# Last layer of a four-layer recurrent model: wide projections among the head pairs, decays ahead of the second query copy, two groups of state inputs on GpSimd

## The chip, the cores and the metric

One core of one Trainium2 chip runs the whole kernel, all in float32. The metric is the time of one execution on the device in microseconds (us). TensorE is PE in the rows, its weight loads are PEld, VectorE is DVE, ScalarE is ACT, GpSimd is POOL, and SyncE, which only issues transfers here, is SP.

## The reference

Sixteen sequences of 256 rows and 128 columns go through four layers, each of which is `x = x + s * silu(f)`. Only the last layer is touched. There `xn = layernorm(x)`, `s` is a state-space block and `f` is a small transformer block:

```
# s: d_inner = 256, 16 states, rank 64
u, z   = split(xn @ in_proj.T)               # the wide projections
xs     = silu(causal_conv4(u) + conv_b)
dt,B,C = split(xs @ x_proj.T)                # 64 + 16 + 16 rows
delta  = softplus(softplus(dt @ dt_proj + dt_b) + dt_b)
state  = exp(delta * -exp(A_log)) * state + (delta * xs) * B   # one step of time
s      = ((state . C + xs * D) * silu(z)) @ out_proj.T
# f: 16 heads of 8, 8 experts of 512, top 2
q,k,v  = xn @ Wqkv + b ; q,k rotated
x1     = layernorm(xn + softmax(q k.T / sqrt(8)) v @ Wo + bo)
f      = layernorm(x1 + sum of the two chosen experts of x1)
```

## The kernel before

The last layer takes the second half of the time. It works on one sequence at a time, 16 in all, in a loop of four passes with four sequences written out in each. Every engine has its program in the order in which it is written, and engines meet at semaphores; nothing else decides the order. While sequence n runs, the parts of n+1 that depend on its input alone are made ahead. One round has these stages:

- **Pairs.** The 16 heads are taken in 8 pairs. For pair p PE makes the transposed scores (`scoresT`, line 2316, nine rows of the array in use), ACT takes their exponential (`exp_scores`, line 2518), and PE multiplies by the values, one block of two pairs at a time (`heads_out`, line 2374). ACT also makes the decays, exp(delta * A), that the scans need: 16 states in four groups of four, two halves (i) of the 256 channels, so eight calls of `decays` (line 2510), each with four activations. `exp_scores(n, p)` ends with one of them. PE turns the next sequence's normed rows here (`turn_x`, line 2247, behind pair 5). Meanwhile DVE scans groups 0 and 1 (`scan`, line 2811) and multiplies by C (`times_c`, line 2821).
- **Between.** The heads' outputs are turned (line 2412), DVE divides by the sums, then follow the output projection (line 2423), a layer norm on DVE and POOL that gives `x1`, the turning of `x1` (line 2430), and the router. PE also has `project_uz` here: the causal convolution as four shifted products for u (line 2257) and z (line 2261).
- **Experts.** Eight experts, up (line 2386) and down (line 2397); DVE adds them and does groups 2 and 3 of the state. `project_dt` makes dt for n+1.
- **Heads.** q and k of n+1 are turned (line 2284), the scores are made (line 2302), and DVE takes the maximum of each row, in four blocks (`heads_max`, line 2780). The negative maximum is written beside q, and q is turned again with it (`copy_qm`, line 2471), so that the exponential needs no bias. Around it DVE and ACT make the double softplus (`softplus_sum`, line 2739) and du = delta * xs (line 2755).
- **Closing.** DVE makes ym, the output of the scan after the gate (its last instruction is line 2918, which raises `ym_ready`), then `state_input` for groups 0 and 1 of n+1 (line 2787, two halves each), and then waits for th_z (tanh of f's half) and for `s_taken`, ACT's copy of the output product (line 2585). With both it updates x (lines 2923, 2926 and 2929). The next round opens with `norm_stats` of the new rows, `scan(0, 0)`, and `norm_rows` (line 2687), which waits for the inverse deviation that POOL takes as a power (line 94).

`scan` works in place on `st[i]`, which `state_input` has filled with du times B. B and C come as rows that SP spreads over all partitions into `bct`; `bct_read` tells SP that a group's slot is free again.

Of the kernel before, what the change touches and what calls it, by code (L numbers as in the profile page):

```python
# [2081 lines left out]
def layer3(nc, c):  # L2082
    w = c.w3
    with ExitStack() as ctx:
# [140 lines left out]
        delta_ready = sem("delta_ready")  # L2225
        dA_ready = sem("dA_ready")
# [14 lines left out]
        def _(pe):  # L2241
# [12 lines left out]
            def project_uz():  # L2254
                for i in range(CI):
                    for k in range(DCONV):
                        done = nc.tensor.matmul(bank[:, 2, i * T:(i + 1) * T], u_projT[:, i, k, :], xpad[:, k:k + T],
                                                start=(k == 0), stop=(k == DCONV - 1))
                done.then_inc(u_in_psum, 1)
                for i in range(CI):  # L2260
                    done = nc.tensor.matmul(bank[:, 3, i * T:(i + 1) * T], z_projT[:, i, :], xnT,
                                            start=True, stop=True)
                done.then_inc(z_in_psum, 1)
# [8 lines left out]
            def project_dt(m):  # L2272
                pe.wait_ge(xdbl_ready, m + 1)
                pe.wait_ge(zg_ready, m + 1)
# [83 lines left out]
            project_uz()  # L2358
# [3 lines left out]
            with pe.Fori(0, NSEQ // 4) as m:  # L2362
                for q in range(4):
# [26 lines left out]
                    def down(e):  # L2390
                        pe.wait_ge(hid_ready, 2 * E3 * n + 2 * e + 2)
                        pe.wait_ge(acc_taken, E3 * n + e + 1)
                        if e == 1:
                            pe.wait_ge(logits_taken, n + 1)
# [20 lines left out]
                    pe.wait_ge(xnT_ready, n + 2)  # L2415
                    qkv_rows(0)
                    pe.wait_ge(y_ready, n + 1)
                    for a in range(TILES):
                        done = nc.tensor.transpose(bank[:, 4, a * P:(a + 1) * P], y[:, a, :], c.ident[:, :])
                    done.then_inc(yT_in_psum, 1)  # L2420
                    pe.wait_ge(yT_ready, n + 1)
                    for a in range(TILES):
                        done = nc.tensor.matmul(bank[:, 5, a * D:(a + 1) * D], yT[:, a * P:(a + 1) * P], w.o[:, :],
                                                start=True, stop=True)
                    done.then_inc(o_in_psum, 1)
                    project_uz()
                    qkv_rows(1)
                    pe.wait_ge(x1_ready, n + 1)
                    for a in range(TILES):
                        done = nc.tensor.transpose(bank[:, 4, a * P:(a + 1) * P], x1[:, a, :], c.ident[:, :])  # L2430
                    done.then_inc(x1T_in_psum, 1)
                    pe.wait_ge(x1T_ready, n + 1)
                    for a in range(TILES):
                        done = nc.tensor.matmul(bank[:, 5, a * E3:(a + 1) * E3], x1T[:, a * P:(a + 1) * P], w.g[:, :],
# [28 lines left out]
        def _(act):  # L2463
# [16 lines left out]
            def silu_uz(m, par):  # L2480
                act.wait_ge(u_in_psum, m + 1)
                for i in range(CI):
                    done = v.activation(xs[:, par, i, :], bank[:, 2, i * T:(i + 1) * T], ACT.Silu,
# [524 lines left out]
```

## Time and profile before

| | |
|---|---|
| median of 3 runs | 2950.62 us (2947.14 to 2953.3) |
| the profiled execution | 2951.83 us, span 2950.1 us |
| mean granted TensorE clock over the span | 0.854 |
| busy: PE, DVE, ACT, POOL | 85%, 79%, 57%, 11% of the span |

The span is the time between the first and the last instruction, so 1.7 us lie around it. The clock is given as the share of 2.4 GHz: 1.00 is 2.4 GHz and 0.50 is 1.2 GHz, and values between are stretches with some of both.

### The profile page before, as it was taken

The page shows a single profiled execution, that of the slowest core. Times are in us where ns is not written, and L with a number is a line of the kernel's source. Part 1 is how long each engine was busy: PE and PEld are TensorE (multiplying, and loading weights), DVE is VectorE, ACT ScalarE, POOL GpSimd, SP SyncE. Part 2 cuts the span into 40 slices and gives each one's busy share as a digit, 9 for nine tenths or more (in the row PEclk, how much of TensorE's full clock was granted, in tenths as well). Part 3 has the DMA queues.
Part 4 walks back from the last instruction along what each step waited for, and adds up shares of the span by engine and source line. Part 5 has one row for each costly group of instructions (what it writes and reads, how often), then busy time and mean ns, then how long its engine had stood idle before and what let it go on. Part 6 is the DMA issues. An engine that isn't in the chain of part 4 may idle for free. (4 is left out here: it accounts for less than half of the span.)

```text
span 2950.1 us, 55763 instructions
## 1 busy us (share of the span) xinstructions
PE 2500.4 (85%) x18940; PEld 1896.2 (64%) x18940; DVE 2327.4 (79%) x6064; ACT 1689.7 (57%) x3432; POOL 336.4 (11%) x357
## 2 busy tenths in 40 slices
PE   1899998899999999776649888888988888888886
PEld 1666666677777777655636666666665666666665
DVE  1899998788788888675257888888888888888887
ACT  1677776556565566443326565655656565565654
POOL 0000000000000000033121111111111111111111
PEclk9999999899999999888858777788776778877777
DMA  7000000000000000210214323343433334443334
GB/s 220 2 0 0 0 0 0 1 2 0 1 0 1 0 1 0 64 27 27 58 55 106 93 73 86 88 108 94 108 87 75 88 89 107 95 102 84 76 91 110
DMA packets 86524, 163.77 MB, mean 56 GB/s; under 512 B 18856, under 2 KB 45617, under 8 KB 86321
## 3 DMA queue, kind: packets, MB, share of 16 engines
q0 software_dynamic: 20480, 62.93, 11.2%
q1 hardware_dynamic: 64640, 98.15, 10.3%
q8 instruction: 94, 1.54, 0.2%
q14 instruction: 110, 0.89, 0.1%
q10 hardware_dynamic: 1200, 0.27, 0.1%
HBM read 92.60 MB, written 9.99 MB: 35 GB/s over the span
## 5 line engine op out<-in xcount | busy, mean ns | idle before, releaser
L1140 ACT ACTIVATE b_neg<-b_neg,b_nmax 128x128 f32<-128x128 f32 (+1 forms) x512 | 190.9, 444 | 205.6 <-DVE b_nmax L1294 205.6
L2548 ACT ACTIVATE d_probs<-l_bank,w_b 128x256 f32<-128x256 f32 x512 | 210.8, 469 | 155.6 <-PE l_bank L2386 153.3
L2811 DVE TENSOR_TENSOR_SCAN d_state<-w,d_state 128x1024 f32<-128x1024 f32 x128 | 290.9, 2284 | 3.8 <-issue 3.4
L2386 PE MATMUL l_bank<-xnT,w_w 128*128 128x256 f32 x1024 | 245.1, 382 | 13.8 <-ACT d_probs L2548 13.8
L2397 PE MATMUL l_bank<-w_w,d_probs 128*128 128x128 f32 x2048 | 252.6, 276 | 0.0
L2397 PEld LDWEIGHTS l_bank<-w_w,d_probs 128*128 128x128 f32 x2048 | 244.9, 192 | 11.7 <-ACT d_probs L2548 5.3
L2316 PE MATMUL l_bank<-w 9*128 9x256 f32 x1040 | 208.8, 669 | 25.5 <-ACT w L2471 18.9
L2510 ACT ACTIVATE w<-d_delta,w_A_log 128x255 f32<-128x255 f32 x520 | 220.2, 498 | 0.0
L94 POOL TENSOR_TENSOR ln_rstd<-ln_var_eps,minus_half 128x2 f32<-128x2 f32 x51 | 70.6, 1384 | 1293.1 <-DVE ln_var_eps L88 1293.1
L2386 PEld LDWEIGHTS l_bank<-xnT,w_w 128*128 128x128 f32 x1024 | 184.7, 190 | 40.5 <-ACT d_probs L2548 20.7
L2316 PEld LDWEIGHTS l_bank<-w 9*128 9x128 f32 x1040 | 123.7, 320 | 96.0 <-issue 32.3
L1294 DVE CUSTOM_DVE_ANT_0 b_neg<-l_bank,causal 128x128 f32<-128x128 f32 (+1 forms) x512 | 151.9, 353 | 32.3 <-PE l_bank L989 16.4
L2780 DVE TENSOR_REDUCE d_qk<-l_bank 128x8 f32<-128x2048 f32 x68 | 152.7, 2288 | 5.5 <-PE l_bank L2302 4.5
L2821 DVE TENSOR_TENSOR d_state<-d_state,d_bct 128x1024 f32<-128x1024 f32 x128 | 151.1, 1222 | 6.3 <-issue 2.7
L1015 PEld LDWEIGHTS l_bank<-down,b_fused 128*128 128x128 f32 x1024 | 123.9, 191 | 50.1 <-issue 29.8
L2302 PE MATMUL l_bank<-w 8*128 8x256 f32 x1088 | 113.1, 562 | 48.5 <-ACT w L2477 25.0
L1015 PE MATMUL l_bank<-down,b_fused 128*128 128x128 f32 x1024 | 148.2, 288 | 6.9 <-DVE b_y L1326 6.3
L2787 DVE TENSOR_TENSOR d_state<-d_bct,d_du 128x1024 f32<-128x1024 f32 x132 | 153.9, 1218 | 0.1
L2616 POOL DMA_DIRECT2D d_state<-d_state x96 | 85.6, 1046 | 588.9 <-DVEq L2823 476.5
L2374 PE MATMUL l_bank<-d_probs,d_vaug 128*32 128x256 f32 x1024 | 123.9, 634 | 30.9 <-ACT d_probs L2518 30.9
L2471 ACT ACTIVATE w<-l_bank 128x1024 f32<-128x1024 f32 x34 | 34.8, 1024 | 198.8 <-PE l_bank L2284 198.8
L2518 ACT ACTIVATE d_probs<-l_bank 128x1024 f32<-128x1024 f32 x130 | 132.1, 1016 | 24.1 <-PE l_bank L2316 24.1
(404 smaller groups left out, 5699.2 us busy)
## 6 DMA issues: line engine op xcount, KB each, us to landing
d_bct<-l_bc SPq DMA_DIRECT2D x132, 512.0 KB, 4.0
d_state<-d_state POOLq DMA_DIRECT2D x96, 512.0 KB, 6.7
d_state<-d_state POOLq DMA_DIRECT2D x32, 256.0 KB, 4.0
x_sorted<-x SPq DMA_DIRECT2D x1, 2560.0 KB, 16.7
w<-in_L_ffn_w_dram SPq DMA_DIRECT2D x1, 2048.0 KB, 10.3
w_w<-in_L_ffn_W_dram SPq DMA_DIRECT2D x1, 2048.0 KB
c2e_xg<-x_sorted SPq DMA_DIRECT2D x16, 128.0 KB
y_sorted<-c2e_yo SPq DMA_DIRECT2D x16, 128.0 KB, 1.8
```

What stands on the lines that cost most here:

```text
L1015: done = nc.tensor.matmul(bank[:, 7, a * D:(a + 1) * D], fused[:, e % 2, f * T + a * P:f * T + (a + 1) * P], c.down1[:, e, f, :], start=(f ...
L1140: done = nc.scalar.activation(neg[:, slot, cols], neg[:, slot, cols], ACT.Exp, bias=nmax[:, slot, a:a + 1], scale=-1.0)
L1294: done = v.tensor_tensor_reduce(neg[:, slot, lo:hi], bank[:, 1 + b, lo:hi], c.causal[:, lo:hi], -SCALE, 3e38, ALU.add, ALU.min, nmax[:, sl ...
L2316: done = nc.tensor.matmul(back[:, 2 * (p % 2) + i, j * T:(j + 1) * T], kT[own, blk, j * P:(j + 1) * P], qT[own, blk, :], start=True, stop= ...
L2386: done = nc.tensor.matmul(bank[:, b, i * T:(i + 1) * T], w.w1[:, e, k * P:(k + 1) * P], x1T[:, :], start=True, stop=True)
L2397: done = nc.tensor.matmul(bank[:, 4 + e % 2, a * D:(a + 1) * D], hid[:, e % 2, k, a * P:(a + 1) * P], w.w2[:, e, k, :], start=(k == 0), st ...
L2510: done = v.activation(dA[i][:, g % (NG - 1), k, 1:T], delta[:, i, 1:T], ACT.Exp, scale=negA[:, i, SG * g + k:SG * g + k + 1])
L2548: done = v.activation(hid[:, e % 2, k, :], bank[:, b, i * T:(i + 1) * T], ACT.Gelu, bias=w.b1[:, e, k:k + 1])
L2780: v.tensor_reduce(qk[:, :, 0, GR * blk:GR * (blk + 1), HD3].rearrange("p a h -> p h a"), banks.rearrange("p h (a t) -> p h a t", a=TILES), ...
L2787: done = v.tensor_tensor(st[i][:, SG * g:SG * (g + 1), :], bct[:, g, :, :], du[:, i, :].unsqueeze(1).to_broadcast([P, SG, T]), ALU.mult)
L2811: done = v.tensor_tensor_scan(group, dA[i][:, g % (NG - 1), :, :].rearrange("p m t -> p (m t)"), group, 0.0, ALU.mult, ALU.add)
L2821: done = v.tensor_tensor(group, group, bct[:, g, :, :], ALU.mult)
```

## The change

Four things are done to the last layer.

1. `project_uz` is cut into `project_u(0)`, `project_u(1)` and `project_z`, which stand behind the scores of pairs 5, 6 and 7. They write to banks 4 and 5 of PSUM instead of 2 and 3, and other small results trade places with them. `turn_x`, whose result they need, moves from behind pair 5 to behind pair 3.
2. The four calls of `decays` for groups 0 and 1 stand in front of `copy_qm`. Of the eight pairs only every second one still carries a call, for groups 2 and 3.
3. For that, `delta` is made sooner: the second `softplus_sum` moves from behind the fourth block of `heads_max` to behind the first.
4. `state_input` of groups 0 and 1 goes from DVE to POOL, where it waits for `ym_ready`, since it overwrites what ym is made of. `scan(0, 0)` and `scan(1, 0)` wait for it.

```diff
-            def project_uz():
+            def project_u(i):
+                for k in range(DCONV):
+                    done = nc.tensor.matmul(bank[:, 4, i * T:(i + 1) * T], u_projT[:, i, k, :], xpad[:, k:k + T],
+                                            start=(k == 0), stop=(k == DCONV - 1))
...
@@ PE, pairs
+                        if k == 3:
+                            turn_x(n + 1, 1 - par)
                         if k == 5:
-                            turn_x(n + 1, 1 - par)
+                            pe.wait_ge(xnT_ready, n + 2)
+                            project_u(0)
+                        if k == 6:
+                            project_u(1)
+                        if k == 7:
+                            project_z()
...
@@ PE, behind the output projection
                     done.then_inc(o_in_psum, 1)
-                    project_uz()
                     qkv_rows(1)
...
@@ ACT
                              scale=float(HD3) ** -0.5).then_inc(probs_ready, 1)
-                decays(n, p // 2, p % 2)
+                if p % 2:
+                    decays(n, 2 + p // 4, p // 2 % 2)
...
                     log_part(n + 1, 1)
+                    for k in range(4):
+                        decays(n + 1, k // 2, k % 2)
                     copy_qm(n + 1)
...
@@ POOL
+            def state_input(m, g):
+                pool.wait_ge(bct_loaded[g], 32 * m + 16)
+                pool.sem_inc(pool_step, 1)
+                for i in range(CI):
+                    nc.gpsimd.tensor_tensor(st[i][:, SG * g:SG * (g + 1), :], bct[:, g, :, :],
+                                            du[:, i, :].unsqueeze(1).to_broadcast([P, SG, T]), ALU.mult)
+                nc.gpsimd.drain().then_inc(bct_read[g], 1)
+                pool.sem_inc(input_ready, 1)
...
                     inner_power(2 * n + 2)
+                    pool.wait_ge(du_ready, n + 2)
+                    pool.wait_ge(ym_ready, n + 1)
+                    for g in range(2):
+                        state_input(n + 1, g)
...
@@ DVE
             def third_part(m, par):
-                softplus_sum(m, 1)
-                v.tensor_tensor(du[:, :, :], delta[:, :, :], xs[:, par, :, :], ALU.mult)
+                v.tensor_tensor(du[:, :, :], delta[:, :, :], xs[:, par, :, :], ALU.mult).then_inc(du_ready, 1)
...
                         dve.wait_ge(dA_ready, CI * NG * n + CI * g + i + 1)
+                        if g < 2 and i == 0:
+                            dve.wait_ge(input_ready, 2 * n + g + 1)
...
                         heads_max(n + 1, blk)
+                        if blk == 0:
+                            softplus_sum(n + 1, 1)
...
-                    for g in range(2):
-                        state_input(n + 1, g)
                     dve.wait_ge(th_z_ready, n + 1)
```

**PE in the pairs.** Before, from the output product of the scan (line 2325) to the turning of the heads' outputs (line 2412). `l_bank` is PSUM, line 2316 is `scoresT`, 2374 is `heads_out`, 2247 is `turn_x`.

```order
L2325 MATMUL l_bank<-d_out_projT,d_ym 128x128 x4
L2316 MATMUL l_bank<-w 128x256 x4
L2374 MATMUL l_bank<-d_probs,d_vaug 32x256 x8
L2316 MATMUL l_bank<-w 128x256 x4
L2316 MATMUL l_bank<-w 128x256 x4
L2374 MATMUL l_bank<-d_probs,d_vaug 32x256 x8
L2316 MATMUL l_bank<-w 128x256 x4
L2247 MATMUL l_bank<-ident,d_xn 128x128 x2
L2316 MATMUL l_bank<-w 128x256 x4
L2374 MATMUL l_bank<-d_probs,d_vaug 32x256 x8
L2316 MATMUL l_bank<-w 128x256 x4
L2374 MATMUL l_bank<-d_probs,d_vaug 32x256 x8
```

The same place in the changed kernel, from behind the first `heads_out`; its lines 2321, 2381 and 2249 are the 2316, 2374 and 2247 of before, and 2258 and 2265 are u and z.

```order
L2321 MATMUL l_bank<-w 128x256 x4
L2249 MATMUL l_bank<-ident,d_xn 128x128 x2
L2321 MATMUL l_bank<-w 128x256 x4
L2381 MATMUL l_bank<-d_probs,d_vaug 32x256 x8
L2321 MATMUL l_bank<-w 128x256 x4
L2258 MATMUL l_bank<-d_xpad,d_u_projT 128x256 x4
L2321 MATMUL l_bank<-w 128x256 x4
L2381 MATMUL l_bank<-d_probs,d_vaug 32x256 x8
L2258 MATMUL l_bank<-d_xpad,d_u_projT 128x256 x4
L2321 MATMUL l_bank<-w 128x256 x4
L2265 MATMUL l_bank<-d_xpad,d_z_projT 128x256 x2
L2381 MATMUL l_bank<-d_probs,d_vaug 32x256 x8
```

`turn_x` now stands between the scores of pairs 3 and 4, which were neighbours, and ten wide products stand between the later ones.

**POOL from the closing of a round into the next.** `until` is the layer norm's small memory, `ln_rstd` the inverse deviation that `norm_rows` needs; lines 2617 and 2618 of the changed kernel are 2598 and 2599 of before.

```order
+L2617 REGISTER_ALU
+L2618 TENSOR_TENSOR until<-until,minus_half 128x2
+L2623 ISA
+L2626 TENSOR_TENSOR d_state<-d_bct,d_du 128x1024 x4
 L93 REGISTER_ALU
 L94 TENSOR_TENSOR ln_rstd<-ln_var_eps,minus_half 128x2
```

The four products of `state_input` now stand ahead of the power for `norm_rows` in POOL's program.

**ACT in heads and closing.** The changed kernel, from the second softplus to the copy for `s_taken` (2604); 2524 is `decays`, 2485 `copy_qm`, 2532 `exp_scores`.

```order
L2514 ACTIVATE d_dneg<-d_dneg 128x512
L2516 ACTIVATE d_dneg<-d_dneg 128x512
L2524 ACTIVATE w<-d_delta,w_A_log 128x255 x16
L2485 ACTIVATE w<-l_bank 128x1024
L2600 ACT_TABLE_LOAD
L2600 ACTIVATE d_x<-same_head 128x256
L2532 ACTIVATE d_probs<-l_bank 128x1024
L2532 ACTIVATE d_probs<-l_bank 128x1024
L2524 ACTIVATE w<-d_delta,w_A_log 128x255 x4
L2604 ACTIVATE xnT<-l_bank 128x256
```

Sixteen of the activations stand ahead of `copy_qm`, where there were none, and four instead of eight stand between the first exponential and the copy for `s_taken`.

## Rows read from the trace of the kernel before

**Rows 1.** Stretches of one round: busy PE, PEld, DVE, ACT, POOL, granted clock, DMA.

```profile
2500.49:2586.51 86.02, 74.88 (x476) 55.73 (x476) 73.96 (x139) 50.45 (x98) 12.38 (x12) 0.76 0.38 93
2502.53:2523.03 20.50, 18.63 (x115) 9.06 (x114) 18.29 (x21) 19.33 (x40) 2.65 (x1) 0.50 0.14 52
2533.82:2567.57 33.75, 32.47 (x214) 28.99 (x212) 28.19 (x71) 19.57 (x42) 5.30 (x6) 1.00 0.59 146
```

**Rows 2.** Timeline of PE in that round: start, us, [idle before <-releaser].

```profile
2502.53 2.08 PE L2316 MATMUL l_bank<-w 9*128 9x256 f32 x8
2504.54 1.94 PE L2374 MATMUL l_bank<-d_probs,d_vaug 128*32 128x256 f32 x16
2506.40 2.45 PE L2316 MATMUL l_bank<-w 9*128 9x256 f32 x16
...
2513.48 0.69 PE L2247 MATMUL l_bank<-ident,d_xn 128*128 128x128 f32 x2
2514.10 2.08 PE L2316 MATMUL l_bank<-w 9*128 9x256 f32 x8
...
2521.17 1.94 PE L2374 MATMUL l_bank<-d_probs,d_vaug 128*32 128x256 f32 x16 [1.12 <-ACT d_probs L2518]
```

**Rows 3.** Timeline of ACT around the closing.

```profile
2497.24 1.02 ACT L2471 ACTIVATE w<-l_bank 128x1024 f32<-128x1024 f32 x1 [9.82 <-PE l_bank L2284]
...
2501.36 1.69 ACT L2510 ACTIVATE w<-d_delta,w_A_log 128x255 f32<-128x255 f32 x4
2502.96 1.00 ACT L2518 ACTIVATE d_probs<-l_bank 128x1024 f32<-128x1024 f32 x1
...
2505.46 0.37 ACT L2585 ACTIVATE xnT<-l_bank 128x256 f32<-128x256 f32 x1
```

**Rows 4.** Timeline of DVE, heads, closing and the next round's opening.

```profile
2486.18 9.00 DVE L2780 TENSOR_REDUCE d_qk<-l_bank 128x8 f32<-128x2048 f32 x4
2495.10 0.68 DVE L2739 SCALAR_TENSOR_TENSOR d_delta<-d_dv,d_dneg 128x512 f32<-128x512 f32 x1
...
2500.38 4.63 DVE L2787 TENSOR_TENSOR d_state<-d_bct,d_du 128x1024 f32<-128x1024 f32 x4
2505.93 0.42 DVE L2923 SCALAR_TENSOR_TENSOR d_y<-d_x,same_head 128x256 f32<-128x256 f32 x1 [0.92 <-ACT xnT L2585]
...
2508.28 2.29 DVE L2811 TENSOR_TENSOR_SCAN d_state<-w,d_state 128x1024 f32<-128x1024 f32 x1
2511.09 0.60 DVE L2687 TENSOR_SCALAR d_xn<-x,ln_meanvar,ln_rstd 128x128 f32 x2 [0.52 <-POOL ln_rstd L94]
...
2525.83 0.37 DVE L2845 RECIPROCAL until<-l_bank 128x16 f32<-128x16 f32 x2 [2.27 <-PE l_bank L2412]
```

**Rows 5.** Timeline of POOL in the same round.

```profile
2508.41 2.65 POOL L94 TENSOR_TENSOR ln_rstd<-ln_var_eps,minus_half 128x2 f32<-128x2 f32 x1 [23.08 <-DVE ln_var_eps L88]
...
2530.71 0.71 POOL L2599 TENSOR_TENSOR until<-until,minus_half 128x2 f32<-128x2 f32 x1 [4.73 <-DVE until L2764]
2531.39 0.72 POOL L2595 TENSOR_TENSOR xn<-d_xn,w_bo 128x256 f32<-128x256 f32 x1
```

**Rows 6.** POOL's groups by form, whole span: count, busy us, mean ns.

```profile
L721 POOL TENSOR_TENSOR a_hbias<-a_hneg,a_hrstd 128x2 f32<-128x2 f32 x16 | 3.2, 197 | 2.3
```

**Rows 7.** DVE's L2769, beside POOL's L2595 and without it.

```profile
2531.45 1.00 DVE L2769 TENSOR_SCALAR same_head<-same_head,until 128x128 f32<-128x128 f32 x2 [0.31 <-POOL until L2599]
...
2582.52 0.59 DVE L2769 TENSOR_SCALAR same_head<-same_head,until 128x128 f32<-128x128 f32 x2
```

**Rows 8.** L2257, product for u: before the first round, and in a round.

```profile
1516.97:1518.25 1.28, 1.28 (x4) 1.01 (x3) 0.50 0.00 0
2528.85:2532.31 3.46, 3.46 (x16) 2.84 (x16) 1.00 0.98 250
```

**Rows 9.** PE between two stages: busy, then the granted clock, DMA, GB/s.

```profile
2525.30:2528.70 3.40, 2.93 (x10) 0.50 0.96 181
2529.70:2533.80 4.10, 4.10 (x19) 1.00 0.62 178
```

More of the change, by code:

```diff
@@ L2252, in qkv_rows, with project_z @@
                     .then_inc(qkv_in_psum, 1)
-            def project_uz():
-                for i in range(CI):
[L2256 to L2261, printed above, removed]
+            def project_u(i):
+                for k in range(DCONV):
+                    done = nc.tensor.matmul(bank[:, 4, i * T:(i + 1) * T], u_projT[:, i, k, :], xpad[:, k:k + T],
+                                            start=(k == 0), stop=(k == DCONV - 1))
+                if i == CI - 1:
+                    done.then_inc(u_in_psum, 1)
+            def project_z():
+                for i in range(CI):
+                    done = nc.tensor.matmul(bank[:, 5, i * T:(i + 1) * T], z_projT[:, i, :], xnT,
                                             start=True, stop=True)
@@ L2273, in project_dt @@
                 pe.wait_ge(xdbl_ready, m + 1)
-                pe.wait_ge(zg_ready, m + 1)
+                if later(m):
+                    pe.wait_ge(logits_taken, m)
                 for i in range(CI):
@@ L2418, in _ @@
                     for a in range(TILES):
-                        done = nc.tensor.transpose(bank[:, 4, a * P:(a + 1) * P], y[:, a, :], c.ident[:, :])
+                        done = nc.tensor.transpose(bank[:, 2, a * P:(a + 1) * P], y[:, a, :], c.ident[:, :])
                     done.then_inc(yT_in_psum, 1)
@@ L2429, in _ @@
                     for a in range(TILES):
-                        done = nc.tensor.transpose(bank[:, 4, a * P:(a + 1) * P], x1[:, a, :], c.ident[:, :])
+                        done = nc.tensor.transpose(bank[:, 2, a * P:(a + 1) * P], x1[:, a, :], c.ident[:, :])
                     done.then_inc(x1T_in_psum, 1)
@@ L2433, in _ @@
                     for a in range(TILES):
-                        done = nc.tensor.matmul(bank[:, 5, a * E3:(a + 1) * E3], x1T[:, a * P:(a + 1) * P], w.g[:, :],
+                        done = nc.tensor.matmul(bank[:, 3, a * E3:(a + 1) * E3], x1T[:, a * P:(a + 1) * P], w.g[:, :],
                                                 start=True, stop=True)
@@ L2482, in silu_uz @@
                 for i in range(CI):
-                    done = v.activation(xs[:, par, i, :], bank[:, 2, i * T:(i + 1) * T], ACT.Silu,
+                    done = v.activation(xs[:, par, i, :], bank[:, 4, i * T:(i + 1) * T], ACT.Silu,
                                         bias=w.conv_b[:, i:i + 1])
@@ L2486, in silu_uz @@
                 act.wait_ge(z_in_psum, m + 1)
-                v.activation(zg[:, par, :, :].rearrange("p i t -> p (i t)"), bank[:, 3, :], ACT.Silu)\
+                v.activation(zg[:, par, :, :].rearrange("p i t -> p (i t)"), bank[:, 5, :], ACT.Silu)\
                     .then_inc(zg_ready, 1)
@@ L2534, in _ @@
             log_part(0, 1)
+            for k in range(4):
+                decays(0, k // 2, k % 2)
             copy_qm(0)
@@ L2578, in _ @@
                     log_part(n + 1, 1)
+                    for k in range(4):
+                        decays(n + 1, k // 2, k % 2)
                     copy_qm(n + 1)
@@ L2629, in _ @@
                     inner_power(2 * n + 2)
+                    pool.wait_ge(du_ready, n + 2)
+                    pool.wait_ge(ym_ready, n + 1)
+                    for g in range(2):
+                        state_input(n + 1, g)
         @block.sync
@@ L2798, in _ @@
                 heads_max(0, blk)
+                if blk == 0:
+                    softplus_sum(0, 1)
             third_part(0, 0)
-            v.drain()
-            for g in range(2):
-                state_input(0, g)
             v.drain()
@@ L2854, in _ @@
                     dve.wait_ge(resid_ready, n + 1)
-                    v.tensor_tensor(rows[:, :, :], bank[:, 5, 0:TILES * D].rearrange("p (a d) -> p a d", d=D),
+                    v.tensor_tensor(rows[:, :, :], bank[:, 3, 0:TILES * D].rearrange("p (a d) -> p a d", d=D),
                                     resid[:, :, :], ALU.add).then_inc(rows_ready, 1)
@@ L2918, in _ @@
                     v.tensor_tensor(ym[:, :, :], ym[:, :, :], zg[:, par, :, :], ALU.mult).then_inc(ym_ready, 1)
-                    for g in range(2):
-                        state_input(n + 1, g)
                     dve.wait_ge(th_z_ready, n + 1)
```

24 lines of the change are left out of this document (16 added, 8 removed).

## The prediction

> **What bounds the kernel now.** I first cut one round of the last layer out of the trace (the table of stretches), then read the timelines of PE, ACT, DVE and POOL over it, since the average over the span hides which engine is last in which stage. A round is 86.02 us, and over it PE is busy 74.88, DVE 73.96, ACT 50.45 and POOL 12.38 us [rows 1]. PE and DVE are both nearly full, so the reader should ask stage by stage who waits for whom, not who is busiest.
>
> Let 2500.5 us, the end of ym, be 0. Pairs: from the third scores to the end of the last `heads_out` is 20.50 us. PE is busy 18.63 of it and ACT 19.33, PE's clock is at 0.50 (1.2 GHz) all through, and PE's last wait, 1.12 us, is for ACT [rows 1, 2]. DVE is the one with room: it waits 2.27 us for the turned outputs at 25.3 [rows 4]. So the stretch from 0 to there is set by PE and ACT in turn, and DVE's work beside it is hidden by 2.27 us. Experts: PE is busy 32.47 of 33.75 us at clock 1.00 and bounds [rows 1]. Heads: DVE's four maxima run without a gap for 9.00 us and bound [rows 4]. Closing: DVE makes the state inputs in 4.63 us and then still waits 0.92 us for ACT's copy [rows 4].
>
> **The change part by part.**
>
> Earlier `softplus_sum` (0.68 us, about 0.7 with the drain behind it [rows 4]): it goes in between the maxima and is missing behind them, so ym ends when it did, but the last maximum comes 0.7 later, and with it the second turning, `copy_qm`, and the first scores. Cost at the start of the pairs: +0.7.
>
> Half of the decays ahead of `copy_qm`: a call takes 1.60 us (start of one to start of what follows, 2501.36 to 2502.96 [rows 3]), four take 6.4. `delta` is ready at 2486.18 + 2.25 + 0.7 = 2489.1 (one of four maxima is 2.25), so they end at 2495.5. `copy_qm` began at 2497.24 after 9.82 us of idle [rows 3], and would now at 2497.9. The idle hides them with 2.4 us over. Free.
>
> Fewer decays in the closing: ACT's copy for `s_taken` had two calls ahead of it and now has one: -1.6 + 0.7 puts its end at about 2504.9 where it was 2505.8 [rows 3]. DVE therefore starts the update of x 0.9 earlier, though 4.63 us of work left it. The rest becomes idle: what was removed from DVE here covered a wait.
>
> State inputs on POOL. No such product of 1024 elements is in the trace. POOL takes 0.72 us for 256 elements, one operand spread [rows 5], and 0.197 for 2 [rows 6], so 2.06 ns an element and 2.3 us for 1024. Bounds: 1.2 us, DVE's price for it (4.63/4 [rows 4]), and 2.9, four times 0.72. I take 2.3. Group 0 then runs from 0.1 to 4.7, and with drain and waits group 1 from 4.9 to 9.5, if nothing holds it. Behind these in POOL's program stands the power for `norm_rows` [rows 5], behind that `norm_rows`, and behind that `turn_x` on PE. SP's loads of C wait for the same products to be done with B: they start 2.6 (group 0) and up to 6 us (group 1) later, while the scans and `times_c` that need them move by about 4 themselves. I count nothing for them.
>
> Does DVE hold POOL up, and POOL DVE? The power on two elements took 2.65 us under a scan that ran from 2508.28 to 2510.57 (it ended at 2511.06, 0.49 behind the scan), but 0.71 where no scan ran [rows 4, 5]. The other way round, DVE's two scalings took 1.00 us beside POOL's addition and 0.59 without it [rows 7]. So each waits the other out. The Trainium skill, "SBUF — State Buffer", "SBUF: two separate sides", says that the port pair of the two is an exclusive lock for the whole instruction, against DVE instructions with two inputs from SBUF as well. By that rule the trace agrees in both directions, and the sum is the one with holding, below; by a reading in which POOL never holds such a DVE instruction the sum would be 4.1 us a round less.
>
> With holding: DVE's update of x is three instructions of 0.43, the first at 4.5. It waits for POOL's second product (4.7), runs to 5.2, POOL takes 2.3, the second runs, POOL takes 2.3, the third ends at 10.6. Statistics and issue up to the scan are 1.0 (2505.93 to 2508.28 less three starts of 0.45), the scan 2.3: about 14.0. The power ends 0.5 later and two scalings take 0.6 [rows 4]: the normed rows are there at 15.1, against 11.2 before. Without holding: POOL free at 9.5, power 0.7, scalings 0.6, and some issue, so 11.0. The scan stands in front anyway.
>
> When does PE want them? Before, `turn_x` ran at 13.0 [rows 2] and waited for nothing. Now it stands behind pair 3: third scores at 2.0 + 0.7 = 2.7, +2.0, `heads_out` +1.9, scores +2.0 = 8.6. PE stands still for 6.5 us (2.4 without holding).
>
> The rest of the pairs on PE, start to start: `turn_x` 0.6, scores 2.0 each, `heads_out` 1.9 each [rows 2]. Adjacent scores of pairs 3 and 4 overlapped (both in 2.45 plus a wait), which `turn_x` between them ends. The new products: four instructions at clock 0.50 begin within 1.28 us, so 0.427 each, against 0.216 at 1.00 [rows 8]. u is 16 of them, z 4: 3.4 for each half of u and 1.7 for z at 1.2 GHz. From `turn_x`: 0.6 + 2.0 + 1.9 + 2.0 = 6.5; then 3.4 + 2.0 + 1.9 + 3.4 + 2.0 + 1.7 + 1.9 = 16.3. End at 15.1 + 22.8 = 37.9. Before it was 22.5. That is +15.4 with the clock low throughout.
>
> The clock. The grant rose right behind a stretch in which PE was busy 2.93 of 3.40 us with turnings and products over the full array [rows 9], and stays at 0.50 through nine-row scores and `heads_out` [rows 1]. u(0) and u(1) are such full stretches of 3.4 us, but each is followed by nine-row scores. If the grant rises behind u(0), the 12.9 us behind it halve: -6.4; behind u(1), -2.5; never, 0. I take half, a quarter and a quarter: -3.8.
>
> Between: u and z leave a place where PE was busy 4.10 of 4.10 us [rows 9]. It delayed the turning of x1 by 0.4, so -0.4, and no more, since DVE's layer norm ran beside it. But only one product of 0.7 is left there, so the clock may be low when the experts begin. PE would lose half of a stretch as long as that from the first full-array work at 23.3 to the rise at 28.2, 4.9/2 = 2.4. I take half: +1.2. Removing u and z from the experts' stage saves nothing, as they were not in it.
>
> Sum for a round: 15.4 (this holds +0.7 and the wait of 6.5) - 3.8 - 0.4 + 1.2 = +12.4. Sixteen rounds: +198. On the profiled execution, 2951.8 us (1.2 above the median of the runs shown), it gives 3150.
>
> **The rivals.**
>
> *The two engines do not hold each other* (POOL's products only delay the power behind them). The wait at `turn_x` is 2.4: 12.4 - 4.1 = 8.3 a round, 3085. For it: the trace shows DVE held only with its scalings, not with a two-input instruction. Against it: the power held by the scan, all of its length.
>
> *The clock rises at the first wide product and stays* (-6.4, and +0 for the experts). 15.4 - 6.4 - 0.4 = 8.6, 3089; with the first rival too 4.5, 3024. For it: 3.4 us of full-array work. Against: the scores behind it. Its opposite, a clock that stays low in the pairs and starts low in the experts, is 17.4, 3230. The Trainium skill, "TensorE: Matmul & The Clock Gate", "HAM oscillation — how this bites in real kernels", describes such falling back when short bursts alternate with pauses; with only that, the sum would be near the 3230, and no run here shows it yet for the pairs.
>
> *Faster: the relief of DVE and ACT is what counts.* The wide products go into PE's waits. DVE's 4.63 a round off the whole is 74 us, 2877. For it: DVE is as full as PE over a round, and ACT's decays stand between the exponentials that PE waits for. Against: PE has 1.9 us of idle in 20.5 in the pairs, and gets 8.5 at 1.2 GHz. It decides if the last `heads_out` ends by 22.5, which needs about 2.4 GHz from the first scores and normed rows by 8.6.
>
> *No change.* The savings and the costs cancel: 2951.
>
> **How the numbers follow.** The forecast 0.55, no holding 0.15, the clock early (with or without holding) 0.15, all low 0.05, faster 0.06, same 0.04. Range 3040 to 3220: it takes in both middle rivals with 3089, most of the case with both (3024 lies outside), and of the high case all but the worst. About 0.2% is what a measurement of this kernel can tell from no change: faster 0.06, same 0.04, slower 0.90.
>
> **What the profile after would show.** Right: POOL's line 2626 with 4 instructions a round of about 2.3 us, some longer where a scan or the update holds them; `turn_x` (2249) with some 6 us of idle before it, released by the normed rows; the update of x split by POOL's products; u and z at about 0.43 an instruction in half of the cases; a pairs stretch above 30 us. ACT's sixteen decays inside the idle time of the maxima. Wrong if POOL's products take under 1.5 us, if the clock is 1.00 through the pairs, if `turn_x` waits under 2 us, or if the experts' stretch begins at 1.00 in all rounds; each takes its term out of the sum.

## The result, and the profile after

The changed kernel takes 3148.22 us (median of 4, 3146.94 to 3151.67), the kernel before in the same runs 2949.72. The ratio is 1.0674, interval 1.0655 to 1.0692: slower by 198 us. The profiled execution of the changed kernel has a span of 3149.9 us. From one end of ym to the next, a round took 86.50 us on average before (15 intervals) and takes 98.81 now, +12.3.

The round looked at from here on starts at 2534.57, the end of ym. Its stretches, against those of [rows 1] (us, busy PE, PEld, DVE, ACT, POOL, granted clock, DMA share, GB/s):

```profile
2534.57:2633.75 99.18, 79.03 (x480) 57.83 (x478) 70.73 (x135) 50.94 (x98) 21.95 (x16) 0.74 0.33 81
2537.25:2569.24 31.99, 26.00 (x135) 14.30 (x134) 17.75 (x18) 13.06 (x26) 11.63 (x7) 0.57 0.27 66
2569.24:2579.21 9.97, 3.54 (x19) 2.07 (x19) 6.79 (x19) 3.94 (x8) 1.40 (x2) 0.96 0.16 53
2579.21:2614.61 35.40, 34.93 (x213) 31.00 (x214) 28.58 (x71) 19.66 (x41) 5.06 (x6) 0.91 0.54 136
2614.61:2633.75 19.14, 11.88 (x102) 8.64 (x104) 17.60 (x27) 12.05 (x23) 1.51 (x2) 0.63 0.16 28
```

The pairs (second row) went from 20.50 to 31.99 us; PE is idle for 6 of them and ACT for 19. The experts (fourth row) went from 33.75 to 35.40, and their clock from 1.00 to 0.91. Those two stretches hold the loss. The timeline of PE over the pairs and the place behind them answers to [rows 2]:

```profile
2537.25 2.08 PE L2321 MATMUL l_bank<-w 9*128 9x256 f32 x8
2539.25 1.94 PE L2381 MATMUL l_bank<-d_probs,d_vaug 128*32 128x256 f32 x16
2541.12 2.08 PE L2321 MATMUL l_bank<-w 9*128 9x256 f32 x8
2549.12 0.69 PE L2249 MATMUL l_bank<-ident,d_xn 128*128 128x128 f32 x2 [5.93 <-DVE d_xn L2722]
...
2555.62 3.78 PE L2258 MATMUL l_bank<-d_xpad,d_u_projT 128*128 128x256 f32 x8
2559.33 2.08 PE L2321 MATMUL l_bank<-w 9*128 9x256 f32 x8
2561.34 1.94 PE L2381 MATMUL l_bank<-d_probs,d_vaug 128*32 128x256 f32 x16
2563.21 2.78 PE L2258 MATMUL l_bank<-d_xpad,d_u_projT 128*128 128x256 f32 x8
2565.92 1.13 PE L2321 MATMUL l_bank<-w 9*128 9x256 f32 x8
...
2579.21 0.69 PE L2444 MATMUL l_bank<-ident,d_x 128*128 128x128 f32 x2 [4.58 <-DVE d_x L2809]
2580.37 1.02 PE L2448 MATMUL l_bank<-w_g,xnT 128*128 128x8 f32 x4 [0.47 <-ACT xnT L2584]
2581.25 3.76 PE L2393 MATMUL l_bank<-xnT,w_w 128*128 128x256 f32 x8
```

`turn_x` waits 5.93 us for the normed rows. u(0) takes 3.7 us; within u(1) the clock rises, and the scores behind it take 1.13 us instead of 2.08. The turning of x1 comes after 4.58 us of idle, and the first product of the experts takes 3.76 us where the ones behind it take 1.89. What POOL and DVE do meanwhile answers to [rows 4, 5]:

```profile
2534.90 4.67 POOL L2626 TENSOR_TENSOR d_state<-d_bct,d_du 128x1024 f32<-128x1024 f32 x2 [15.58 <-DVE d_ym L2955]
2540.60 6.83 POOL L2626 TENSOR_TENSOR d_state<-d_bct,d_du 128x1024 f32<-128x1024 f32 x2 [1.02 <-issue]
2547.74 0.69 POOL L94 TENSOR_TENSOR ln_rstd<-ln_var_eps,minus_half 128x2 f32<-128x2 f32 x1 [0.32 <-issue]
```
```profile
2539.22 0.64 DVE L2958 SCALAR_TENSOR_TENSOR d_y<-d_x,same_head 128x256 f32<-128x256 f32 x1 [4.65 <-ACT xnT L2604]
...
2541.66 1.43 DVE L88 TENSOR_SCALAR ln_var_eps<-ln_meanvar 128x2 f32<-128x2 f32 x1
2543.01 2.28 DVE L2846 TENSOR_TENSOR_SCAN d_state<-w,d_state 128x1024 f32<-128x1024 f32 x1
2548.47 0.60 DVE L2722 TENSOR_SCALAR d_xn<-x,ln_meanvar,ln_rstd 128x128 f32 x2 [3.18 <-POOL ln_rstd L94]
...
2571.37 0.37 DVE L2880 RECIPROCAL until<-l_bank 128x16 f32<-128x16 f32 x2 [10.38 <-PE l_bank L2428]
```

POOL's first two products take 4.67 us, undisturbed. The second pair takes 6.83: the scan of 2.28 us ran inside it. DVE is idle for 4.65 us in the closing, where the state inputs stood, and for 10.38 later.

### The profile page after: what moved, and what is told of

It is laid out like the page before. It is cut to its first block, busy times and chain, and to the rows that moved or that the text cites. A ratio compares the mean times of both kernels' runs of the same rounds, so it can differ in the third digit from the quotient of the medians.

```text
span 3149.9 us, 55927 instructions
## 1 busy us (share of the span) xinstructions
PE 2559.7 (81%) x18940; PEld 1927.7 (61%) x18940; DVE 2269.3 (72%) x5996; ACT 1702.6 (54%) x3444; POOL 499.9 (16%) x425
## 4 chain that ended last, share of the span: by engine, by line
PE 19%; issue 10%; DVE 9%; DVEq 5%; POOL 4%; POOLq 3%; ACT 1%; ACTq 0%
PE l_bank L2393 8%; PE l_bank L2406 7%; DVE d_qk L2814 4%; POOLq L2628 3%; POOL d_state L2626 3%; DVEq L2852 2%; DVE d_state L2856 1%; DVEq L2858 1%; DVE d_state L2846 1%; POOL d_state L2647 1%; PE l_bank L2272 1%; DVE same_head L2803 1%; PE l_bank L2281 1%; POOL ln_rstd L94 1%; PE l_bank L2448 1%
## 5 line engine op out<-in xcount | busy, mean ns | idle before, releaser
L2393 PE MATMUL l_bank<-xnT,w_w 128*128 128x256 f32 x1024 | 272.6, 414 | 0.0
L2321 PE MATMUL l_bank<-w 9*128 9x256 f32 x1040 | 218.9, 633 | 23.8 <-ACT w L2485 18.9
L2626 POOL TENSOR_TENSOR d_state<-d_bct,d_du 128x1024 f32<-128x1024 f32 x68 | 187.1, 2770 | 299.0 <-DVE d_ym L2955 248.1
L2393 PEld LDWEIGHTS l_bank<-xnT,w_w 128*128 128x128 f32 x1024 | 204.7, 209 | 27.6
L94 POOL TENSOR_TENSOR ln_rstd<-ln_var_eps,minus_half 128x2 f32<-128x2 f32 x51 | 47.3, 927 | 904.1 <-DVE ln_var_eps L88 899.9
L1294 DVE CUSTOM_DVE_ANT_0 b_neg<-l_bank,causal 128x128 f32<-128x128 f32 (+1 forms) x512 | 152.0, 353 | 34.7 <-PE l_bank L989 18.8
L997 PE MATMUL l_bank<-b_xnT,gating 128*128 128x256 f32 x512 | 135.0, 387 | 3.3 <-DVE b_gated L1311 3.3
L1003 PE MATMUL l_bank<-b_xnT,up 128*128 128x256 f32 x512 | 133.1, 383 | 0.0
```

The lines of the kernel that those rows point to most:

```text
L1294: done = v.tensor_tensor_reduce(neg[:, slot, lo:hi], bank[:, 1 + b, lo:hi], c.causal[:, lo:hi], -SCALE, 3e38, ALU.add, ALU.min, nmax[:, sl ...
L2321: done = nc.tensor.matmul(back[:, 2 * (p % 2) + i, j * T:(j + 1) * T], kT[own, blk, j * P:(j + 1) * P], qT[own, blk, :], start=True, stop= ...
L2393: done = nc.tensor.matmul(bank[:, b, i * T:(i + 1) * T], w.w1[:, e, k * P:(k + 1) * P], x1T[:, :], start=True, stop=True)
L2626: nc.gpsimd.tensor_tensor(st[i][:, SG * g:SG * (g + 1), :], bct[:, g, :, :], du[:, i, :].unsqueeze(1).to_broadcast([P, SG, T]), ALU.mult)
```

## The experiments

The changed kernel and the kernel before were first taken apart part by part; then single terms were tested. All ratios are to the kernel before in the same runs. "Round" and the places in it are medians over the 15 rounds of each profiled execution, in us behind the end of ym; "low" is the time at 1.2 GHz up to the last `heads_out`, and within the experts (from the turning of x1 to the turning of q and k).

| kernel | ratio (interval) | round | normed rows | wait at `turn_x` | last `heads_out` | experts | low: pairs, experts |
|---|---|---|---|---|---|---|---|
| before | 1 | 86.1 | 11.2 | 0 | 22.6 | 33.8 | 22.6, 0 |
| changed | 1.0674 (1.0655 to 1.0692) | 98.9 | 14.5 | 5.9 | 34.7 | 35.5 | 30.2, 6.3 |
| only_pool | 1.0080 (1.0063 to 1.0097) | 87.9 | 14.4 | 1.4 | 24.1 | 33.9 | 24.1, 0 |
| only_decays | 1.0028 (1.0018 to 1.0037) | 86.9 | 10.4 | 0 | 23.3 | 34.0 | 23.3, 0 |
| only_wide | 1.0480 (1.0463 to 1.0498) | 95.6 | 11.2 | 3.3 | 31.4 | 35.5 | 26.9, 6.3 |
| undo_pool | 1.0346 (1.0329 to 1.0363) | 92.2 | 10.4 | 1.8 | 27.8 | 35.6 | 20.2, 6.6 |
| gap_filled | 1.0607 (1.0562 to 1.0651) | 98.8 | 14.5 | 5.9 | 35.8 | 34.1 | 32.7, 0 |
| pairs_filled | 1.0318 (1.0300 to 1.0335) | 92.4 | 14.5 | 0.7 | 27.4 | 36.0 | 13.7, 7.2 |
| power_first | 1.0708 (1.0687 to 1.0728) | 99.4 | 14.7 | 6.2 | 34.9 | 35.4 | 30.4, 6.1 |
| split_groups | 1.0567 (1.0549 to 1.0584) | 96.3 | 12.4 | 3.8 | 32.2 | 36.0 | 27.5, 7.3 |
| late_wide | 1.0115 (1.0098 to 1.0132) | 88.6 | 10.4 | 0 | 26.1 | 34.1 | 22.2, 0 |
| warm_pairs | 0.9963 (0.9950 to 0.9975) | 85.4 | 10.2 | 0 | 22.9 | 34.1 | 13.7, 0 |
| warm_decays | 0.9890 (0.9873 to 0.9906) | 83.9 | 10.2 | 0 | 20.3 | 34.0 | 14.2, 0 |
| fill_only | 0.9970 (0.9957 to 0.9983) | 85.5 | 11.1 | 0 | 22.2 | 33.8 | 18.7, 0 |

**only_pool.** Part 4 of the diff put on the kernel before, nothing else.

> The kernel before with part 4 alone: POOL makes the state inputs of groups 0 and 1. Theory: the products come in front of the power for norm_rows and exclude scan and update, so the normed rows are there at about 14.5 us behind the end of ym instead of 11.2. turn_x stands at 13.0 here, so PE waits 1.5 to 2 us in a round: +24 to +32 us, ratio 1.008 to 1.011. Rival 'POOL's part is what costs': +8 or more in a round, ratio over 1.04. Rival 'relief of DVE counts': ratio 0.975.

1.0080, as the theory has it. The normed rows come 3.2 us later; since `turn_x` stands at 13.0 there, 1.4 us are left as a wait, and that is the loss. Neither rival fits. POOL's part is small by itself, because more than half of its lateness falls before PE asks. In the changed kernel PE waits for the rows in any case, and more of the lateness counts: 5.9 us of wait against 3.3 in only_wide, although the pairs start 0.7 later.

**only_decays.** Parts 2 and 3 on the kernel before.

> The kernel before with parts 2 and 3 alone: decays of groups 0 and 1 ahead of copy_qm, softplus sooner. Theory: pairs start 0.7 us later and PE at 1.2 GHz then paces them alone (18.6 us of work and about 1.5 of waits for exponentials), so a round stays within -0.3 to +0.6 us: ratio 0.998 to 1.003. Rival 'ACT's decays pace the pairs': -1 us or more in a round, ratio under 0.995.

1.0028: a small loss, the 0.7 us by which the last maximum and with it the pairs start later. That ACT has four calls of decays less in the pairs gave nothing.

**only_wide.** Part 1 on the kernel before.

> The kernel before with part 1 alone: wide projections and turn_x in the pairs. Theory: turn_x waits 2.5 to 3 us for the normed rows at 11.2, behind it PE needs 20 us (as in the changed kernel), so heads_out ends at 31.3 instead of 22.6; the experts start at a low clock (+1.7), the place between gives 0.7 back: +9.7 in a round, ratio 1.053 (1.045 to 1.060). Rival 'the products fit into PE's waits': under 1.01.

1.0480, inside the range. `turn_x` waits 3.3 us even with POOL's products absent, since the normed rows stand behind `scan(0, 0)` in any case. The rival (under 1.01) is out. This part alone makes 71% of the loss.

**undo_pool.** The changed kernel without part 4.

```diff
@@ POOL
-                    for g in range(2):
-                        state_input(n + 1, g)
...
@@ DVE, behind ym
+                    for g in range(2):
+                        state_input(n + 1, g)
```

> The changed kernel with the state inputs back on DVE. Theory: normed rows at 10.4 to 11, turn_x waits 2 to 2.5 us instead of 5.9, all else as in the changed kernel: +9.1 in a round against before, ratio 1.049 (1.042 to 1.055), that is 3.5 to 4 us a round faster than the changed kernel. Rival 'POOL's part is what costs': ratio under 1.02. Rival 'no holding, POOL is harmless': ratio as the changed kernel's, 1.067.

1.0346, under the range that I gave, and away from both rivals. The wait is 1.8, a little under what I expected, and from `turn_x` to the last `heads_out` it takes 17.3 us, not 20.1. The timeline shows where:

```profile
2203.78 0.69 PE L2247 MATMUL l_bank<-ident,d_xn 128*128 128x128 f32 x2 [1.84 <-DVE d_xn L2704]
...
2210.28 3.53 PE L2256 MATMUL l_bank<-d_xpad,d_u_projT 128*128 128x256 f32 x8
2213.74 1.13 PE L2319 MATMUL l_bank<-w 9*128 9x256 f32 x8
```

Here the clock rises at the end of u(0), in the changed kernel in the middle of u(1) in most rounds. So the removal of POOL's part gave 4.1 us by the shorter wait and 2.8 by the clock. The second is no property of the part: it depends on when the same products run, and in the two rounds of 96.2 us of the changed kernel, where the clock also rises at the end of u(0), the stretch takes 17.2 us with POOL's part in place. What single parts cost (1.7 + 0.7 + 9.4 = 11.8 us of a round by medians) is near the whole (12.8), but not a sum that can be relied on to 3 us.

**gap_filled.** Tests the low clock at the start of the experts.

```diff
                     done.then_inc(o_in_psum, 1)
+                    for _ in range(5):
+                        nc.tensor.matmul(bank[:, 7, 0:3 * D], xnT[:, P:2 * P], wqkv, start=True, stop=True)
                     qkv_rows(1)
```

> The changed kernel with the product for the second half of q, k, v made six times instead of once, in the place that u and z left behind the output projection (the copies rewrite the same values, so no result changes). They take about 3.9 us of the 5.4 that PE has there. Theory: the low clock at the start of the experts (6.3 us at 1.2 GHz in each round) comes from that empty place; with it filled the clock stays at 2.4 GHz, the stretch from the turning of x1 to the turning of q and k goes from 35.4 to 33.8 us, and a round is 1.6 us shorter: -26 us against the changed kernel, ratio to before 1.058. Rival 'the clock falls there for another reason': no change, 1.067.

The mechanism is confirmed: the stretch that answers to the experts has no time at 1.2 GHz in any round, and takes 34.06 us in the one shown.

```profile
2262.34:2296.40 34.06, 32.53 (x213) 29.05 (x213) 28.51 (x71) 19.39 (x41) 4.79 (x6) 1.00 0.55 141
```

The gain in time, 0.7% of the time before, measures this less well, since the rise in the pairs moved too. Ten rounds are 98.7 to 99.3 us long: there the last `heads_out` came later (35.8 against 34.7), with 32.6 to 33 us at 1.2 GHz up to it, and took most of the gain back. Five are 95.2 to 95.8, with 25.5 to 26 us at 1.2 GHz.

**pairs_filled.** Tests the price of the low clock in the pairs.

```diff
                         if k == 3:
+                            for _ in range(6):
+                                nc.tensor.matmul(bank[:, 5, T:2 * T], z_projT[:, 0, :], xnT, start=True, stop=True)
                             turn_x(n + 1, 1 - par)
```

> The changed kernel with six extra products over the full array (z's first half, into columns that nobody reads until they are written again) ahead of turn_x, 5.1 us at 1.2 GHz in a wait of 5.8. Theory: the clock rises at about the moment turn_x starts. If it holds through the nine-row scores, the stretch from turn_x to the last heads_out goes from 20.1 us to 12 to 13, a round is 7 us shorter, ratio 1.029; if the scores take it down again before u(0), it rises again behind u(0) as in undo_pool (17.3 us), 2 to 4 us shorter, ratio 1.045 to 1.056. Rival 'the low clock does not matter there, exponentials or the normed rows pace the pairs': under 1 us, ratio 1.065 or more.

1.0318: more work on PE, and 105 us less than the changed kernel. From `turn_x` to the last `heads_out`:

```profile
2310.10:2322.83 12.73, 12.66 (x102) 7.72 (x102) 11.34 (x7) 7.45 (x14) 0.19 (x1) 1.00 0.00 1
```

In this round the clock rose just ahead of `turn_x` and held through the nine-row scores; the same products take 12.73 us at 1.00 and 20.1 in the changed kernel. So it is in 11 of the 15 rounds, and there the first of my two cases is the right one. In the other four the clock fell again at 16.3 to 17.4 us behind ym, among the scores, and the stretch took 16.0 to 19.2. This execution took 3055.55 us, the three others 3041.43 to 3043.67.

**power_first.** Is it POOL's queue, or the holding?

```diff
@@ POOL, top of the round
-                    norm_power(nc, c, s, n + 1)
...
@@ POOL, end of the round
-                    for g in range(2):
-                        state_input(n + 1, g)
+                    state_input(n + 1, 0)
+                    norm_power(nc, c, s, n + 2)
+                    state_input(n + 1, 1)
```

> The changed kernel with the power for norm_rows between POOL's two groups instead of behind both (the order in its program; nothing is left out). Theory 'place in POOL's queue and holding': the power runs at about 7.4 or is held by the scan until 9.6, normed rows at 10 to 12 instead of 14.5, the second group of state inputs then alternates with scan(0, 1) and times_c(0), hidden by DVE's 10 us of idle time before the turned outputs. turn_x waits 1.5 to 3 instead of 5.8: a round 3 to 4 us shorter, and up to 3 more if the clock then rises a step earlier as in undo_pool: ratio 1.035 to 1.050. Rival 'holding alone': the products hold DVE's update and scan wherever they stand, normed rows at 13 or later, ratio over 1.058.

My theory fell and the rival stands: 1.0708, normed rows at 14.7. DVE:

```profile
2449.88 2.29 DVE L2847 TENSOR_TENSOR_SCAN d_state<-w,d_state 128x1024 f32<-128x1024 f32 x1
2452.69 4.66 DVE L2723 TENSOR_SCALAR d_xn<-x,ln_meanvar,ln_rstd 128x128 f32 x2 [0.52 <-POOL ln_rstd L94]
```

and POOL, in the same round:

```profile
2449.94 2.72 POOL L94 TENSOR_TENSOR ln_rstd<-ln_var_eps,minus_half 128x2 f32<-128x2 f32 x1 [2.43 <-DVE ln_var_eps L88]
2452.63 4.63 POOL L2626 TENSOR_TENSOR d_state<-d_bct,d_du 128x1024 f32<-128x1024 f32 x2
```

The power is done 10.2 us behind ym and not 13.9 as in the changed kernel, and the two scalings that it releases, 0.60 us of work, take 4.66, the length of POOL's second group (4.63). The order in POOL's program changed only which instruction was held.

**split_groups.** Does POOL also hold a DVE product with two inputs?

```diff
@@ DVE
                     v.tensor_tensor(ym[:, :, :], ym[:, :, :], zg[:, par, :, :], ALU.mult).then_inc(ym_ready, 1)
+                    state_input(n + 1, 1)
@@ POOL
-                    for g in range(2):
-                        state_input(n + 1, g)
+                    state_input(n + 1, 0)
```

> The changed kernel with group 1 of the state inputs back on DVE (2.4 us, in the closing, where DVE waits 4.65), group 0 on POOL at the same time. Theory 'they hold each other': DVE's two products and POOL's two start together and alternate; POOL's pair takes 6 to 7 us instead of 4.67, or DVE's products some 3.5 us instead of 1.22 each, the update of x starts at about 6 to 7. The power then follows the group at 8 to 10, normed rows at 11 to 12.5: 2 to 3.5 us a round shorter than the changed kernel, ratio 1.040 to 1.055. Rival 'no holding': both groups done by 5, each instruction at its own length, normed rows at 10.5, ratio as undo_pool's, 1.035.

Ratio 1.0567, a little above my range. DVE's and POOL's rows:

```profile
2414.77 4.51 DVE L2819 TENSOR_TENSOR d_state<-d_bct,d_du 128x1024 f32<-128x1024 f32 x2
2419.51 2.27 DVE L2959 SCALAR_TENSOR_TENSOR d_y<-d_x,same_head 128x256 f32<-128x256 f32 x1 [0.23 <-ACT xnT L2604]
```
```profile
2415.18 6.32 POOL L2626 TENSOR_TENSOR d_state<-d_bct,d_du 128x1024 f32<-128x1024 f32 x2 [15.57 <-DVE d_ym L2955]
```

DVE's two products take 4.51 us instead of 2.3 (four took 4.63 [rows 4]), POOL's 6.32 instead of 4.67, and the first instruction of the update 2.27 instead of 0.42. One by one, DVE's first product keeps its 1.22 us although POOL's first begins 0.4 us into it; POOL's first then takes 3.02, DVE's second 3.38, POOL's second 3.32. So they take turns; had they shared a rate, DVE's first product would have been slowed too. Both directions, for instructions with two inputs from SBUF: what the prediction took from scalings alone is shown. The Trainium skill, "SBUF — State Buffer", "SBUF: two separate sides", says that whichever instruction starts first gets the shared ports to its end, and the other engine fully blocks. The trace agrees: the first instruction of the update, begun at 2419.51, ended 0.3 us behind POOL's second product.

**late_wide and warm_pairs.** undo_pool with the projections placed later, without and with products that raise the clock before the pairs. ACT's copy of the turned rows moves one pair down with `turn_x`, which the cut of the diff leaves out.

```diff
@@ late_wide, against undo_pool
-                        if k == 3:
-                            turn_x(n + 1, 1 - par)
                         if k == 5:
-                            pe.wait_ge(xnT_ready, n + 2)
-                            project_u(0)
+                            turn_x(n + 1, 1 - par)
                         if k == 6:
-                            project_u(1)
+                            pe.wait_ge(xnT_ready, n + 2)
+                            project_u(0)
                         if k == 7:
-                            project_z()
+                            project_u(1)
...
                     done.then_inc(o_in_psum, 1)
+                    project_z()
+                    for _ in range(3):
+                        nc.tensor.matmul(bank[:, 7, 0:3 * D], xnT[:, P:2 * P], wqkv, start=True, stop=True)
@@ warm_pairs, against late_wide, in attention_front
+                pe.wait_ge(max_ready, NBLK * n + NBLK - 1)
+                for _ in range(3):
+                    nc.tensor.matmul(bank[:, 6, 0:T], z_projT[:, 0, :], xnT, start=True, stop=True)
                 pe.wait_ge(max_ready, NBLK * n + NBLK)
                 turn_heads(0, bank[:, 4:6, :]).then_inc(qmT_in_psum, 1)
+                for _ in range(2):
+                    nc.tensor.matmul(bank[:, 6, 0:T], z_projT[:, 0, :], xnT, start=True, stop=True)
```

> undo_pool with turn_x behind pair 5 again, u(0) behind pair 6, u(1) behind pair 7, z behind the output projection and three more copies of the q, k, v product there. Theory: no wait at turn_x, scores of pairs 3 and 4 adjacent again; the work of PE from the third scores to the last heads_out is 18.6 + 6.8 us at 1.2 GHz, less what a clock rising behind u(0) gives back: last heads_out at 27 to 30 (before 22.6), experts at 2.4 GHz from their start. +3.5 to +6 a round against before: ratio 1.019 to 1.033. Rival 'the wait at turn_x was the whole loss': ratio 1.00.

> late_wide with the extra products of warm_decays at the end of the heads stage. Theory: these bring the clock up before the pairs. If it holds through them, the last heads_out is at 18 to 20, DVE (free at 22.2) is last, and a round is 2 to 3 us shorter than before: ratio 0.968 to 0.980. If it falls within the pairs: as late_wide, 1.02 to 1.035.

late_wide came out at 1.0115, better than I gave: with no wait at `turn_x` and the experts at 2.4 GHz from their start, 2.5 us of a round are left. I put them down to u in the pairs, where the last `heads_out` comes 3.4 us later; no run takes u out alone. warm_pairs, 0.9963, lies between my two cases: the clock is up at the start of the pairs and falls within them (13.7 us low).

**warm_decays and fill_only.** The products ahead of the pairs, on only_decays and on the kernel before. The diff is the last hunk above.

> only_decays with extra products over the full array on PE at the end of the heads stage: three beside the last maximum, two behind the second turning of q (into a bank that is free there; no result changes). Theory: with the decays moved, PE at 1.2 GHz paces the pairs; a clock of 2.4 GHz at their start lets ACT pace them (8 exponentials of 0.9, 4 calls of decays of 1.6, two copies: about 15 us instead of 20.5), until DVE, free at 22.2, is last. If the clock holds: a round 3 us shorter than before, ratio 0.965. If the nine-row scores take it down within the pairs: the 0.6 us that the copies delay the first scores are left, ratio 1.000 to 1.010.

> The kernel before with the extra products of warm_decays and nothing else. Theory: with a call of decays behind each exponential, ACT paces the pairs (19.3 us of work in 20.5), so a higher clock at their start gives little and the copies ahead of the first scores cost 0 to 0.6 us a round: ratio 0.998 to 1.004. Rival 'the clock alone makes warm_decays faster, the moved decays have no part in it': ratio 0.990 or less.

warm_decays is faster than both kernels: 2917.32 us (2914.93 to 2920.53) against 2949.31 before in the same runs. Its 0.9890 lies between my two cases (0.965 if the clock holds, 1.000 to 1.010 if it falls): the clock falls, 2.7 to 7.7 us behind ym in every round, but what it gave until then was more than I had counted. The table shows what changed in a round: 14.2 us at 1.2 GHz in the pairs where the kernel before has 22.6, and a last `heads_out` 2.4 earlier. One round, whose ym ends at 2651.5: the stretch before the clock falls, and a later one.

```profile
2650.07:2658.50 8.43, 7.60 (x82) 4.65 (x82) 7.95 (x16) 8.42 (x15) 0.00 (x0) 1.00 0.31 116
2658.50:2671.50 13.00, 10.42 (x62) 4.89 (x58) 12.02 (x9) 8.26 (x15) 2.65 (x1) 0.50 0.02 8
```

At 1.00 ACT is busy all the time and paces the pairs; at 0.50 it is idle for 5 of 13 us, and PE, busy for 10.4, is the fuller of the two. In 7 of the 15 rounds, this one among them, PE also waits 1.4 to 1.7 us for the normed rows at `turn_x`. fill_only gives 0.3%, so neither half does it alone: the decays moved cost 0.28%, the clock alone gives 0.30, together 1.1. fill_only is a little under my range: its rival, that the clock alone explains warm_decays, is out all the same.

## Why the prediction was right

The forecast was 3150 us, the measured time 3148. The sum for a round was +12.4; the mean round grew by 12.3. By terms, for the round shown:

- **Start of the pairs**, +0.7. The third scores begin 2.7 us behind ym, as worked out.
- **Decays ahead of the second copy**, free. They take 6.47 us (6.4 given) and ACT still waits 2.52 us behind them (2.4 given). The 0.7 us that only_decays costs in a round is the later start of the pairs, so nothing is left for the decays.
- **DVE's relief covered a wait.** DVE's idle time before the update grew from 0.92 to 4.65 us, and of the 4.6 removed nothing reached the round.
- **Price of POOL's product**, 2.3 us: measured 2.33. It was worked out from a row of a quarter of the size and one of two elements.
- **Normed rows** at 15.1, measured 14.5, wait 6.5, measured 5.9. The total is right, the way there less so. Between the groups POOL spent 1.0 us on its drain and waits where I had given 0.2, so the update of x slipped through behind its first instruction; POOL then held the little addition of line 88 (1.43 us instead of 0.17), and the scan held POOL's fourth product. power_first and split_groups show the holding directly. The step "behind these in POOL's program stands the power" was told as a cause beside the holding, and power_first shows that the place in the program does not set the time: with the power moved ahead, the rows are as late.
- **Rest of the pairs**, 22.8 at 1.2 GHz less 3.8 for the clock; measured 20.1, so 2.7 came back. u(1) begins 28.6 us behind ym in most rounds, and the clock rises at 30.0 to 30.4, within it, in twelve of the 15, at 33.6, behind it, in one, and at 24.2, at the end of u(0), in the two rounds of 96.2 us. My shares (half, a quarter, a quarter) were too kind, and the term was mis-sized by 1.1. Its case behind u(1) was also mis-summed: half of the 5.6 us that stand there is 2.8 and not 2.5, which moves the term by less than 0.1. pairs_filled shows that the clock is the right name for it: at 1.00 the same work takes 12.7.
- **Between**, -0.4, measured -0.8 in the round shown and -0.9 by medians: with the clock up, the turnings there are shorter too.
- **Experts**, +1.2 as half of 2.4. It is 1.7 in the round shown and by medians, with 6.1 to 7.8 us at 1.2 GHz in every round; gap_filled shows the cause. The half was a chance where there was none.
- **Heads**, nothing given, +0.2 in the round shown and +0.1 by medians. No run shows why.

In the round shown these terms do not cancel: the errors are -0.6 at the wait, +1.1 and +0.5 at the clock, -0.4 between and +0.2 in the heads, and the round grew by 13.2 where the sum has 12.4. The mean round grew by 12.3 because the sum started from a round of 86.02, while the mean before is 86.50 (three of the 15 rounds take 87.9 to 88.1), and because two rounds of the changed kernel take only 96.2; by medians it is 12.8. That the forecast fell 2 us from the result is luck; that the size and the place were right is not. Of the rivals, "do not hold each other" is refuted by split_groups. The early clock is real, but in this kernel it came in two of 15 rounds; in undo_pool, with other times of the products, it is the rule. Its opposite was right for the experts, which begin at 1.2 GHz in every round, and wrong for the pairs: the clock rose before the last `heads_out` in all 15. "Relief counts" would have needed PE's pairs at 2.4 GHz; pairs_filled is as near to that as the experiments came, and is still slower than before by 3.2%.

One point stays open: why the clock falls early in the pairs in every round of warm_decays and holds to the last `heads_out` in 11 of 15 rounds of pairs_filled. The latter has u and z in between; no run tells whether these hold it. They are not all of it, for in the four rounds where it fell the products were the same and it had risen at 12.9 to 14.0 us, about where it did in the others (13.5 to 13.8).

## What to carry to other kernels

Before work is moved off a busy engine, look at what the engine waits for behind it: here DVE's update of x waited for ACT's copy until 5.4 us behind ym before the change, and taking 4.6 us of products out from in front of it turned them into 4.65 us of idle time. Before it is moved to GpSimd, ask which VectorE instructions run at that moment, since products with two inputs from SBUF did not overlap in split_groups, and two scalings, which read one tensor, were held in power_first as well. The norm's statistics kept their 0.3 us each beside GpSimd's third product, so not everything is held; free time on GpSimd counts only where VectorE waits or runs what it does not hold.

Work that fills a hole on TensorE can be worth more than its own time, because it keeps the clock at 2.4 GHz for what follows; here, taking it away left a hole that cost 1.7 us in the next stage, and putting it into a stage at 1.2 GHz doubled its price (3.8 us instead of 2.0 for a half of u). A result that is wanted earlier needs its inputs earlier too: `turn_x` moved up by 4.4 us, and its rows could not come before the scan that stands in front of them.

## What the runs showed of the hardware

Products that nobody uses made a tuned kernel faster: five at the end of the heads stage, 2.93 and 1.03 us of PE's time in a round of fill_only, on an engine that was already 85% busy, took 0.3% off by themselves and 1.4% off with the decays moved (0.9890 against 1.0028).

GpSimd and VectorE held each other for whole instructions in both directions: a power on two elements took 2.72 us under a scan of 2.29, two scalings of 0.60 took 4.66 beside GpSimd's products, and an addition on two elements took 1.43 instead of 0.17. GpSimd's drain with its semaphore steps cost 1.0 us between two groups.

The time of one unchanged stretch (from `turn_x` to the last `heads_out`) was 20.1, 17.3 and 12.7 us in most rounds of three kernels with the same instructions in it, by when the clock rose. A loss found by undoing one part contains such shifts, here 2.8 of 6.8 us.
